# Attention, online memory and a routed FFN on one core: the merge's end reordered, the experts' slot rows transposed by DMA

## Chip, cores, metric

The kernel runs on one core of a Trainium2 chip. The metric is the device time of one execution in microseconds (us); three runs were taken.

## What is computed

```python
def attn(x, mem, ...):                    # x: 8 x 1024 x 256, already layer-normed; mem: 64 x 256
    x_in = concatenate([mem, x], axis=1)
    out_swa = sliding_window_attention(x_in)                # 4 heads, window 128
    grads = grad(0.5 * sum((mlp(x_in) - out_swa) ** 2))     # silu MLP, 256 -> 1024 -> 256
    out_mem = mlp(updated params, x_in)
    g1, g2 = sigmoid(out_swa @ lin1.T), sigmoid(out_mem @ lin2.T)
    return (g1 * out_swa + g2 * out_mem)[:, 64:]

def ffn(h, ...):                          # 8192 tokens, 8 experts, top 2, capacity 640 per expert
    probs = softmax(h @ gate_w.T + gate_b);  top_p, top_i = top_k(probs, 2)
    for c in range(2):                    # dispatch to slots, expert MLP, gather back
        pos = cumsum(one_hot(top_i[:, c])) - 1 at the chosen expert;  keep = pos < CAP
        xbuf[top_i[:, c] * CAP + pos] = h
        yb = relu(xb @ W1[e] + b1) @ W2[e] + b2
        y += yb[slot] * top_p[:, c] * keep

x = x + attn(layernorm(x));  x = x + ffn(layernorm(x))
```

The routed part cuts its tokens off at CAP = 640 slots per expert and choice, as the kernel's constants have it (ROUTED = 2048 tokens give the capacity).

## The kernel before, in words

Four phases follow each other: attention, gradient, merge, experts. Each is a block with its own instruction stream per engine, and a block ends when every engine has drained. All matmuls in f32 are done as three fp32r products of high and low halves (`matmul_split`, line 105): a high half is a rounded copy, a low half is the rest. Whoever wants to multiply needs both halves; ACT usually makes the high one and DVE or POOL the low one. The order of work on each engine is written out by hand; semaphores (`wait_ge`, `then_inc`) join them.

**Merge** (`merge_phase`) goes over 16 chunks C of 512 tokens. Per chunk: eight hidden tiles (`hidden`, products in three PSUM banks `ps_z`), gate1 from `oT`, the memory output `om` (two halves of 128 rows), gate2 of the chunk before. The tail of chunk C-1 runs inside chunk C: second term, merge, `residual` (transposes back to rows, x1), layer norm (x2), `transpose_x2`, `router` (matmuls to 8 logits), and inside chunk C+1 `choose`, `choose_experts`, `dispatch`: softmax, top 8 of the probabilities, counting matmuls, slot numbers. POOL then scatters each row with `routed.scatter` (line 840, indirect DMA) to `xbuf_d`, a row of 256 values and a tail of 4 (token number, two probabilities). x2 is kept in three rotating buffers `routed.rows` of 260 f32, which the scatters read. The last chunk's tail has nothing to hide in. There ACT (from line 2060) and DVE (from line 2281) do the steps in turn, and then make the halves of the first expert's W1 and W2. The last four scatters of merge (`scatter(NCH - 1, 0)`) follow `dispatch(NCH - 1)` on POOL. The eight scatters of the second choice of the last two chunks are the first work of POOL in the expert phase.

**Experts** (`expert_phase`) has 16 rounds i: choice i // 8, expert i % 8, 640 slots in SB = 5 blocks of 128. Per round TensorE does eight `up` tiles (12 products of 320 columns each, L105 into `e_ps_z`) and `down` for five blocks (24 products of 256 columns each, into `e_ps_y`, two banks). In between it transposes the next round's slot rows (`transpose_slots`, line 2496, into `e_ps_x`): blocks 0 to 3 after the first 24 downs, block 4 before the last 24. ACT takes them out of PSUM as the high half (`round_slots`, line 2558), DVE makes the low one (`rest_slots`, line 2609). SP loads W1, the slots (`load_slots`, line 2696, one DMA of 650 KB per round into one of two `slots` buffers) and W2. POOL gathers the output rows of the slots' tokens, DVE adds the weighed result (`weigh`, line 2631), POOL scatters them back. The first round loads its slots in five DMAs (line 2699) and transposes them in three groups before its first up.

In the gradient phase the hidden rows are transposed by DMA: ACT splits f32 words into planes of 16-bit words (line 1213), SP issues a DMA transpose (line 1631), ACT joins them again (line 1219).

## Time and profile before

| | us |
|---|---|
| three runs | 2437.65, 2439.75, 2441.54 (median 2439.75) |
| profiled execution, its time | 2437.23 |
| its span | 2435.4 |
| mean granted TensorE clock | 0.984 |
| busy: TensorE, DVE, ACT, POOL | 2356.8, 1692.9, 1529.5, 1407.8 |
| expert phase, first slot load to the end of the span | 1955.6 to 2435.4 |

The busy time of TensorE is that of the union of its matmuls, which overlap; the rate at which they follow each other is read from starts, or from the pieces of the chain. The granted clock is 1.00 at 2.4 GHz and 0.50 at 1.2 GHz. A name such as PEq or POOLq is an engine's sequencer: waits, branches, issues, drains.

### The profile page before, as it was taken

The page shows a single profiled execution, that of the slowest core. Times are in us where ns is not written, and L with a number is a line of the kernel's source. Part 1 is how long each engine was busy: PE and PEld are TensorE (multiplying, and loading weights), DVE is VectorE, ACT ScalarE, POOL GpSimd, SP SyncE. Part 2 cuts the span into 40 slices and gives each one's busy share as a digit, 9 for nine tenths or more (in the row PEclk, how much of TensorE's full clock was granted, in tenths as well). Part 3 has the DMA queues.
Part 4 walks back from the last instruction along what each step waited for, and adds up shares of the span by engine and source line. Part 5 has one row for each costly group of instructions (what it writes and reads, how often), then busy time and mean ns, then how long its engine had stood idle before and what let it go on. Part 6 is the DMA issues. An engine that isn't in the chain of part 4 may idle for free. (4 is left out here: it accounts for less than half of the span.)

```text
span 2435.4 us, 40493 instructions
## 1 busy us (share of the span) xinstructions
PE 2356.8 (97%) x15170; PEld 2104.4 (86%) x15170; DVE 1692.9 (70%) x3640; ACT 1529.5 (63%) x2390; POOL 1407.8 (58%) x1000
## 2 busy tenths in 40 slices
PE   7999999799999999999999989999999789999998
PEld 6888888688888888888888878888888679999998
DVE  6787776466666666666666766777777657776776
ACT  4787878657777767777776556666656434333333
POOL 2666566556676666667666634666666553333333
PEclk8999999899999999999999999999999889999999
DMA  3222221533333232233222232333222044444441
GB/s 127 81 88 70 92 74 53 222 103 63 69 77 62 61 66 61 64 68 78 61 61 61 72 106 80 102 99 100 91 86 69 22 154 136 139 148 142 136 137 59
DMA packets 260083, 221.76 MB, mean 91 GB/s; under 512 B 138226, under 2 KB 228759, under 8 KB 259760
## 3 DMA queue, kind: packets, MB, share of 16 engines
q1 hardware_dynamic: 246064, 188.73, 27.2%
q0 software_dynamic: 13824, 30.44, 3.7%
q8 instruction: 120, 1.97, 0.3%
q14 instruction: 75, 0.61, 0.1%
HBM read 123.13 MB, written 72.12 MB: 80 GB/s over the span
## 5 line engine op out<-in xcount | busy, mean ns | idle before, releaser
L2314 POOL TENSOR_TENSOR m_hl<-m_hf,m_hh 128x512 fp32r<-128x512 f32 x112 | 158.5, 1421 | 111.6 <-ACT m_hh L1963 110.1
L2675 POOL DMA_INDIRECT out<-e_ys,slot_token x80 | 83.1, 1039 | 223.6 <-DVE e_ys L2631 214.6
L2564 ACT ACTIVATE e_hf<-e_ps_z,e_b 128x640 f32<-128x640 f32 x128 | 101.9, 796 | 145.8 <-PE e_ps_z L105 145.3
L105 PE MATMUL e_ps_y<-r_w_h,e_hl 128*128 128x256 f32 x640 | 180.3, 282 | 0.0
L840 POOL DMA_INDIRECT xbuf_d<-xn,scatter_rows x128 | 153.0, 1195 | 46.4 <-issue 38.1
L105 PE MATMUL e_ps_y<-r_w_h,e_hh 128*128 128x256 f32 x640 | 178.1, 278 | 0.0
L105 PE MATMUL e_ps_y<-r_w_l,e_hh 128*128 128x256 f32 x640 | 177.9, 278 | 0.0
L1565 POOL TENSOR_TENSOR halves_l<-hT_full,halves_h 128x512 fp32r<-128x512 f32 x120 | 153.6, 1302 | 38.3 <-ACT halves_h L1225 38.3
L701 POOL TENSOR_TENSOR prob<-prob,softmax_small 128x1024 f32<-128x1024 f32 x65 | 123.2, 1896 | 72.1 <-DVE softmax_small L634 72.1
L105 PE MATMUL e_ps_z<-slotsT_h,w_l 128*128 128x320 f32 x512 | 159.2, 311 | 1.3 <-DVE slotsT_l L2609 1.3
L105 PE MATMUL e_ps_z<-slotsT_l,w_h 128*128 128x320 f32 x512 | 159.0, 311 | 0.0
L105 PE MATMUL e_ps_z<-slotsT_h,w_h 128*128 128x320 f32 x512 | 158.9, 310 | 0.0
L1423 DVE TENSOR_TENSOR new_w2T<-g_bank,new_w2T 128x512 f32<-128x512 f32 x128 | 88.6, 692 | 93.8 <-PE g_bank L105 93.8
L1219 ACT ACTIVATE hT_full<-h_wordsT 128x2048 uint16<-128x2048 uint16 x60 | 153.1, 2552 | 0.0
L105 PE MATMUL g_bank<-dpred_h,h_l 128*128 128x256 f32 x520 | 148.0, 285 | 2.9 <-DVE shared_x L1416 2.8
L105 PE MATMUL g_bank<-halves_l,keys_h 128*128 128x256 f32 (+1 forms) x528 | 147.8, 280 | 0.0
L105 PE MATMUL g_bank<-dpred_l,h_h 128*128 128x256 f32 x520 | 147.7, 284 | 0.0
L105 PE MATMUL g_bank<-dpred_h,h_h 128*128 128x256 f32 x520 | 147.7, 284 | 0.0
L105 PE MATMUL g_bank<-halves_h,keys_l 128*128 128x256 f32 (+1 forms) x528 | 147.5, 279 | 0.0
L105 PE MATMUL g_bank<-halves_h,keys_h 128*128 128x256 f32 (+1 forms) x528 | 147.3, 279 | 0.0
L1430 DVE TENSOR_TENSOR new_w1T<-g_bank,new_w1T 128x512 f32<-128x512 f32 x128 | 88.5, 692 | 83.6 <-PE g_bank L105 83.6
L1239 ACT ACTIVATE dpredT_h<-dpredT 128x512 fp32r<-128x512 f32 (+1 forms) x33 | 20.7, 627 | 182.6 <-DVE dpredT L1384 178.5
(318 smaller groups left out, 9024.9 us busy)
## 6 DMA issues: line engine op xcount, KB each, us to landing
shared_x<-in_x SPq DMA_DIRECT2D x32, 512.0 KB, 4.9
shared_xT<-xT_d SPq DMA_DIRECT2D x64, 256.0 KB, 4.6
new_w1T<-in_W SPq DMA_DIRECT2D x16, 1024.0 KB, 5.1
new_w2T<-in_W SPq DMA_DIRECT2D x16, 1024.0 KB, 5.7
xbuf_d<-new_w1T SPq DMA_DIRECT2D x16, 650.0 KB, 8.0
slots<-xbuf_d SPq DMA_DIRECT2D x15, 650.0 KB, 6.8
xn_d<-xn SPq DMA_DIRECT2D x32, 256.0 KB, 2.4
xT_d<-shared_xT SPq DMA_DIRECT2D x32, 256.0 KB, 2.6
```

The lines of the kernel that those rows point to most:

```text
L105: i = e.matmul(out, a, b, start=first and not onto and n == 0, stop=last and n == len(terms) - 1, skip_group_check=onto)
L701: e.tensor_tensor(p[:], p[:], sm[:, 3].unsqueeze(2).broadcast_to([P, HEADS, 2 * P]), ALU.mult).then_inc(*prob_made(g))
L840: e.indirect_dma_start(io["xbuf_d"][k], bass.IndirectOffsetOnAxis(ap=self.slot[C % 2][:, k, j:j + 1], axis=0), self.rows[C % 3][:, j], Non ...
L1219: e.activation(hT_f[b][:].bitcast(U16).rearrange("p (n s) -> p s n", s=2), wordsT[b][:].rearrange("p (s k) t -> p s (k t)", s=2), ACTF.Cop ...
L1239: e.activation(dTh[:, :, 0:N], dpf[:, :, 0:N], ACTF.Copy).then_inc(*dT_high(p))
L1423: e.tensor_tensor(dst, bank("g2", p, t)[:], dst, ALU.add).then_inc(*g2_added(p, t))
L1430: e.tensor_tensor(dst, bank("g1", p, t)[:], dst, ALU.add).then_inc(*g1_added(p, t))
L1565: e.tensor_tensor(hTl[:, ks, block[b]], hT_f[b][:, hc].rearrange("p (k t) -> p k t", k=4), hTh[:, ks, block[b]], ALU.subtract).then_inc(*m ...
L2314: e.tensor_tensor(hl[:, t, 0:N], hf[(HC * C + t) % NZ][:, 0:N], hh[:, t, 0:N], ALU.subtract).then_inc(*h_low(C, t))
L2564: e.activation(hf[(HC * i + t) % NHF][:].rearrange("p (s n) -> p s n", s=2), ps_z[t % 2][:, :, 0:HALF], ACTF.Relu, bias=b1[:, i % E, t:t + ...
L2675: e.indirect_dma_start(io["out"], bass.IndirectOffsetOnAxis(ap=token[i % 2][:, b:b + 1], axis=0), ys[:, b], None, bounds_check=NT - 1, oob ...
```

## The change

Merge. A row in `routed.rows` and in `xbuf_d` becomes 520 words of 16 bits: 256 low words, 256 high words, and the tail of 4 f32 as before; the number of bytes is the same. DVE writes x2 to one f32 buffer, and ACT splits it into the planes (`split_x2`), before the second om in a steady chunk. The router takes the top 8 from the logits, so that the expert search no longer waits for the softmax; `shift` makes the differences for all and for the top two, and `weigh` (sum, reciprocal, product of the top two) takes the place of `choose`. The first term moves from the head of the next chunk to the end of its own. In the last chunk om isn't copied as f32 (DVE reads it from PSUM), gate2 goes to banks of its own, W1's halves for the experts are made earlier, W2's high half earlier on ACT, W2's low half in the expert phase, the dispatch of chunk 14 goes ahead of the second term, the sigmoid's table is loaded in advance, and TensorE gets 52 filling matmuls (`keep_busy`) and 8 more at the start of the experts.

Experts. From round 1 on the slot rows are loaded by five DMA transposes and one DMA for the tails, ACT joins the words and rounds them, DVE makes the low half; TensorE transposes nothing. Round 0 loads plain rows, ACT and DVE join the words, and TensorE transposes as before; the first up's first half waits for two groups only. `weigh(i, 1)` goes ahead of the first `rest_slots`.

```diff
         x1 = [sb("x1_0", [P, GRP, D]), shared.oT[:].rearrange("p (j d) -> p j d", j=GRP)]
-        x2 = routed.rows
+        rows = routed.rows
+        x2 = sb("xn2_full", [P, GRP, D])
...
     def gate2_part(C, n):
...
-        acc = bank("gate2", C, n)[:].rearrange("p (m t) -> p m t", m=KC)
+        acc = part_bank(n)[:].rearrange("p (m t) -> p m t", m=KC)
         pe.wait_ge(*om_low.at(C, 1))
-        pe.wait_ge(*freed("gate2", C, n))
+        pe.wait_ge(*h_made.at(C, HC - 1))
...
-    for n in range(2):
-        gate2_part(NCH - 1, n)
-    for n in range(2):
-        residual(NCH - 1, n)
+    def keep_busy(n):
+        for _ in range(n):
+            e.matmul(ps_z[2][:], shared.keys[0][:, 0:P], shared.keys[0][:, 0:512], start=True, stop=True)
+    gate2_part(NCH - 1, 0)
     dispatch(NCH - 2)
+    gate2_part(NCH - 1, 1)
+    keep_busy(2)
+    residual(NCH - 1, 0)
+    keep_busy(2)
+    residual(NCH - 1, 1)
+    keep_busy(12)
     for n in range(2):
         transpose_x2(NCH - 1, n)
     for n in range(2):
         router(NCH - 1, n)
+    keep_busy(4)
     dispatch(NCH - 1)
+    keep_busy(32)
...
+    def split_x2(C, n):
+        blocks = parts_of(C)[n]
+        act.wait_ge(*x2_made.at(C, n))
+        for k in range(TOPK):
+            act.wait_ge(*routed.landed(k, C - 3))
+        e.activation(rows[C % 3][:, blocks, 0:2 * D].rearrange("p j (s n) -> p j s n", s=2),
+                     x2[:, blocks].bitcast(U16).rearrange("p j (n s) -> p j s n", s=2), ACTF.Copy).then_inc(*x2_split(C, n))
...
+        if C == NCH - 1:
+            for k in range(KC):
+                act.wait_ge(*first_w1.at(0))
+                act.wait_ge(*z_done.at(NCH - 1, HC - 1))
+                e.activation(w1h[:, k], g1[:, k], ACTF.Copy).then_inc(*e_w1_high(k))
...
             copy_x2T(C - 1, 0)
+            split_x2(C - 1, 0)
         memory_out(C, 1)
         if tail:
             exponent(C - 1)
+    act.wait_ge(*const_set.at(1))
+    e.activation(spare[:], neg_half[:, 0:1], ACTF.Sigmoid)
     for n in range(2):
         gate2_part(NCH - 1, n)
-    for k in range(KC):
-        act.wait_ge(*first_w1.at(0))
-        act.wait_ge(*z_done.at(NCH - 1, HC - 1))
-        e.activation(w1h[:, k], g1[:, k], ACTF.Copy).then_inc(*e_w1_high(k))
-    for n in range(2):
-        copy_x2T(NCH - 1, n)
-    exponent(NCH - 1)
     for k in range(2):
         r = slice(4 * k, 4 * k + 4)
         act.wait_ge(*first_w2.at(0))
         act.wait_ge(*om_done.at(NCH - 1, 1))
-        e.activation(w2h[:, r], g2[:, r], ACTF.Copy).then_inc(*e_w2_high(k))
+        e.activation(w2h[:, r], g2[:, r], ACTF.Copy)
+    for n in range(2):
+        copy_x2T(NCH - 1, n)
+    for n in range(2):
+        split_x2(NCH - 1, n)
+    exponent(NCH - 1)
...
     def second_term(C, n):
         cols = columns(parts_of(C)[n])
-        dve.wait_ge(*gate2_made.at(C, n if C == NCH - 1 else 1))
-        e.tensor_tensor(gb[:, :, cols], gb[:, :, cols], om[:, :, cols], ALU.mult).then_inc(*term2(C, n))
+        if C < NCH - 1:
+            dve.wait_ge(*gate2_made.at(C, 1))
+            e.tensor_tensor(gb[:, :, cols], gb[:, :, cols], om[:, :, cols], ALU.mult).then_inc(*term2(C, n))
+            return
+        dve.wait_ge(*gate2_made.at(C, n))
+        for m in range(KC):
+            i = e.scalar_tensor_tensor(gb[:, m, cols], bank("om", C, m)[:, cols], b2n[:, m:m + 1], gb[:, m, cols], ALU.add, ALU.mult)
+        i.then_inc(*term2(C, n))
...
     def norm_apply(C, n):
-        y, z, blocks = x1[C % 2], x2[C % 3], parts_of(C)[n]
+        y, blocks = x1[C % 2], parts_of(C)[n]
         dve.wait_ge(*rstd_made.at(C, n))
+        dve.wait_ge(*x2T_done.at(*final_part(C - 1)))
...
+        for j in range(blocks.start, blocks.stop):
+            i = e.tensor_scalar(x2[:, j], y[:, j], mv[:, j, 0:1], rstd[:, 1, j:j + 1], ALU.subtract, ALU.mult)
+        i.then_inc(*x2_made(C, n))
...
-        for j in range(blocks.start, blocks.stop):
-            i = e.tensor_scalar(z[:, j, 0:D], y[:, j], mv[:, j, 0:1], rstd[:, 1, j:j + 1], ALU.subtract, ALU.mult)
-        i.then_inc(*x2_made(C, n))
...
+        for j in range(n):
+            i = e.max(top[:, j], lg[:, j])
+        i.then_inc(*lg_top(C))
+    def shift(C):
+        n, best = SIZES[C], top[:, 0:SIZES[C], 0:1]
+        dve.wait_ge(*lg_top.at(C))
         dve.wait_ge(*exp_made.at(C - 1))
-        e.tensor_tensor(lg[:, 0:n], lg[:, 0:n], mx[:, 0:n].unsqueeze(2).broadcast_to(wide), ALU.subtract).then_inc(*lg_shifted(C))
-    def choose(C):
-        n, wide = SIZES[C], [P, SIZES[C], E]
+        e.tensor_tensor(below[:, 0:n, 0:E], lg[:, 0:n], best.broadcast_to([P, n, E]), ALU.subtract).then_inc(*shifted(C, 0))
+        e.tensor_tensor(below[:, 0:n, E:], top[:, 0:n, 0:TOPK], best.broadcast_to([P, n, TOPK]), ALU.subtract).then_inc(*shifted(C, 1))
...
+    def weigh(C):
+        n = SIZES[C]
         dve.wait_ge(*exp_made.at(C))
...
+        e.tensor_reduce(sm[:, 0, 0:n], pr[:, 0:n, 0:E], AX.X, ALU.add).then_inc(*weighed(C, 0))
+        dve.wait_ge(*weighed.at(C, 0))
+        e.reciprocal(sm[:, 1, 0:n], sm[:, 0, 0:n]).then_inc(*weighed(C, 1))
+        dve.wait_ge(*weighed.at(C, 1))
         dve.wait_ge(*placed.at(C - 1, 7))
...
+        e.tensor_tensor(top_p[:, 0:n], pr[:, 0:n, E:], sm[:, 1, 0:n].unsqueeze(2).broadcast_to([P, n, TOPK]),
+                        ALU.mult).then_inc(*weighed(C, 2))
...
-                choose(C - 2)
+                weigh(C - 2)
...
+        first_term(C)
+        if C == NCH - 1:
+            for k in range(KC):
+                dve.wait_ge(*e_w1_high.at(k))
+                e.tensor_tensor(w1l[:, k], g1[:, k], w1h[:, k], ALU.subtract)
         rest_om(C, 1)
         if tail:
             router(C - 1)
-    choose(NCH - 2)
+            shift(C - 1)
     choose_experts(NCH - 2)
-    first_term(NCH - 1)
+    weigh(NCH - 2)
+    dispatch(NCH - 2)
     for n in range(2):
         second_term(NCH - 1, n)
         merge(NCH - 1, n)
...
         norm_stats(NCH - 1, n)
     for n in range(2):
         norm_apply(NCH - 1, n)
-    dispatch(NCH - 2)
     router(NCH - 1)
-    choose(NCH - 1)
     choose_experts(NCH - 1)
+    shift(NCH - 1)
+    weigh(NCH - 1)
     dispatch(NCH - 1)
...
     def scatter(C, k):
         pool.wait_ge(*placed.at(C, 7))
         pool.wait_ge(*numbered.at(*final_part(C)))
+        pool.wait_ge(*x2_split.at(*final_part(C)))
         routed.scatter(e, io, k, C)
...
-        xs = [sb(f"slots{i}", [P, SB, ROW]) for i in range(2)]
+        tail = [sb(f"slot_tail{i}", [P, SB, ROW - D]) for i in range(2)]
+        words = [sb(f"slot_words{i}", [P, 2 * KC, CAP], U16) for i in range(2)]
+        xf = sb("slotsT_full", [P, KC, CAP])
+        first_words = words[0][:].rearrange("p a t -> p (a t)").rearrange("p (b n) -> p b n", b=SB)
+        first_rows = xf[:].rearrange("p k t -> p (k t)").rearrange("p (b d) -> p b d", b=SB)
...
+    def transpose_first(n):
+        bs, out = groups[0][n], first_bank(n)
         for a, b in enumerate(bs):
-            if i == 0:
-                pe.wait_ge(*first_in[b].at(0))
+            pe.wait_ge(*(act_joined.at(b) if b in by_act else dve_joined.at(b)))
             for m in range(KC):
-                x = e.transpose(out[:, (a * KC + m) * P:(a * KC + m + 1) * P], xs[i % 2][:, b, m * P:(m + 1) * P], ident[:])
-        x.then_inc(*xT_done(i, n))
+                x = e.transpose(out[:, (a * KC + m) * P:(a * KC + m + 1) * P], first_rows[:, b, m * P:(m + 1) * P], ident[:])
+        x.then_inc(*first_T(n))
...
     def up(i, t):
...
-        pe.wait_ge(*xT_low.at(*final_group(i)))
...
         for s in range(2):
+            pe.wait_ge(*xT_low.at(*((0, 1) if (i, s) == (0, 0) else final_group(i))))
...
+    for _ in range(8):
+        e.matmul(ps_z[0][:, 0], w1h[:, 0, 0:P], w1h[:, 0, 0:512], start=True, stop=True)
     for n in range(len(groups[0])):
-        transpose_slots(0, n)
+        transpose_first(n)
     for i in rounds:
         for t in range(HC):
             up(i, t)
         down(i, 0, 0)
         down(i, 1, 0)
-        if i + 1 < ROUNDS:
-            transpose_slots(i + 1, 0)
         down(i, 0, 1)
         down(i, 1, 1)
         for b in range(2, SB):
-            if i + 1 < ROUNDS and b == SB - 1:
-                transpose_slots(i + 1, 1)
             down(i, b, 0)
...
     def round_slots(i, n):
-        bs, src = group_view(i, n)
-        act.wait_ge(*xT_done.at(i, n))
+        cols = slots_of(i, n)
+        act.wait_ge(*slots_in[i % 2].at(i, SB - 1))
+        act.wait_ge(*xT_low.at(*final_group(i - 1)))
+        if i == 1:
+            act.wait_ge(*first_T.at(len(groups[0]) - 1))
+        e.activation(xf[:].bitcast(U16).rearrange("p k (t s) -> p s k t", s=2)[:, :, :, cols],
+                     words[i % 2][:].rearrange("p (s k) t -> p s k t", s=2)[:, :, :, cols], ACTF.Copy).then_inc(*joined(i, n))
+        act.wait_ge(*joined.at(i, n))
         act.wait_ge(*up_done.at(i - 1, HC - 1))
-        e.activation(xh[:].rearrange("p m (b t) -> p m b t", t=P)[:, :, bs], src, ACTF.Copy).then_inc(*xT_high(i, n))
+        e.activation(xh[:, :, cols], xf[:, :, cols], ACTF.Copy).then_inc(*xT_high(i, n))
...
+    def join_first(b):
+        act.wait_ge(*first_in[b].at(0))
+        e.activation(first_rows[:, b].bitcast(U16).rearrange("p (n s) -> p s n", s=2),
+                     first_words[:, b].rearrange("p (s n) -> p s n", s=2), ACTF.Copy).then_inc(*act_joined(b))
+    def round_first(n):
+        bs, src = first_view(n)
+        act.wait_ge(*first_T.at(n))
+        e.activation(xh[:].rearrange("p m (b t) -> p m b t", t=P)[:, :, bs], src, ACTF.Copy).then_inc(*xT_high(0, n))
...
+    join_first(0)
+    join_first(2)
+    round_first(0)
+    join_first(4)
+    round_first(1)
+    round_first(2)
...
     def rest_w2(i, k):
         r = slice(4 * k, 4 * k + 4)
-        dve.wait_ge(*w2_high.at(i, k))
+        if i:
+            dve.wait_ge(*w2_high.at(i, k))
         e.tensor_tensor(w2l[:, r], s2[:, r], w2h[:, r], ALU.subtract).then_inc(*w2_low(i, k))
...
     def rest_slots(i, n):
-        bs, src = group_view(i, n)
+        cols = slots_of(i, n)
         dve.wait_ge(*xT_high.at(i, n))
+        e.tensor_tensor(xl[:, :, cols], xf[:, :, cols], xh[:, :, cols], ALU.subtract).then_inc(*xT_low(i, n))
...
+    for b in by_dve:
+        join_first(b)
     for n in range(len(groups[0])):
-        rest_slots(0, n)
+        rest_first(n)
     slot_tokens(0)
+    for k in range(2):
+        rest_w2(0, k)
...
+        add_bias(i, 1)
+        weigh(i, 1)
         if i + 1 < ROUNDS:
             rest_slots(i + 1, 0)
-        add_bias(i, 1)
-        weigh(i, 1)
...
+        x = x_v[i // E][i % E]
+        for b in range(SB):
+            if i:
+                e.dma_start(words[i % 2][:, :, b * P:(b + 1) * P], x[:, b, 0:2 * D], transpose=True).then_inc(*slots_in[i % 2](i, b))
+            else:
+                e.dma_start(first_words[:, b], x[:, b, 0:2 * D]).then_inc(*first_in[b](0))
+        e.dma_start(tail[i % 2][:].bitcast(U16), x[:, :, 2 * D:]).then_inc(*tail_in[i % 2](i))
```

## Rows read from the trace of the kernel before

**Rows 1.** Page, part 1: engine, busy us (share of span), instructions.
```profile
PE 2356.8 (97%) x15170; PEld 2104.4 (86%) x15170; DVE 1692.9 (70%) x3640; ACT 1529.5 (63%) x2390; POOL 1407.8 (58%) x1000
```

**Rows 2.** Chain of waits, rounds 14 and 15: start us, us, what.
```profile
2386.02 2.72 PE e_ps_y L105 x24
...
2388.75 0.87 PE e_ps_x L2496 x8
...
2389.62 8.49 PE e_ps_y L105 x72
...
2398.11 0.22 PE e_ps_x L2496 x2
...
2398.32 2.73 PE e_ps_y L105 x24
...
2401.05 14.08 PE e_ps_z L105 x96
...
2415.13 13.61 PE e_ps_y L105 x120
```

**Rows 3.** Stretches: length, busy us by engine, PEclk, DMA share, GB/s.
```profile
1940.00:1950.00 10.00, 1.22 (x18) 1.03 (x17) 7.94 (x35) 2.12 (x3) 5.60 (x5) 0.50 0.03 4
...
2010.00:2040.00 30.00, 30.00 (x236) 30.00 (x235) 22.00 (x37) 11.89 (x15) 11.28 (x10) 1.00 0.42 137
```

**Rows 4.** Timeline, merge chunk: start, us, engine, instruction [idle before <-releaser].
```profile
1877.32 0.48 PE L105 MATMUL m_ps_o<-m_hh,r_w_l 128*128 128x512 f32 x1 [0.32 <-ACT gate L1968]
...
1857.46 0.69 ACT L1987 ACTIVATE memT<-m_ps_o,new_b 128x512 f32<-128x512 f32 x1 [1.76 <-PE m_ps_o L105]
```

**Rows 5.** Tile and line views (ns min/median/max), page part 6 (KB, us).
```profile
L1213 ACT ACTIVATE hT_full<-h_full x60: 1912/1913/1916, 519.9 to 1348.2; 128x2048 uint16<-128x2048 uint16 x60
...
L1631 SPq DMA_TRANSPOSE h_wordsT<-hT_full x60: 1317/1890/3135, 521.8 to 1350.1; - x60
...
L1219 ACT ACTIVATE hT_full<-h_wordsT x60: 2529/2551/2574, 529.3 to 1356.3; 128x2048 uint16<-128x2048 uint16 x60
...
DMA to landing us min/median/max: 4.2/4.3/6.0
...
new_w1T<-in_W SPq DMA_DIRECT2D x16, 1024.0 KB, 5.1
...
new_w2T<-in_W SPq DMA_DIRECT2D x16, 1024.0 KB, 5.7
```

**Rows 6.** Timeline of TensorE and DVE at the merge's end.
```profile
1935.29 2.12 PE L1893 MATMUL m_ps_r<-r_ident,xn 128*128 128x128 f32 x8 [3.43 <-DVE xn L2160]
...
1937.20 3.47 PE L1903 MATMUL m_ps_s<-gate_w,xn2T 128*128 128x8 f32 x16
...
1936.22 0.28 DVE L2216 TENSOR_TENSOR router_pos_e<-m_ps_s,expert_counts 128x32 f32<-128x32 f32 x2
...
1937.63 0.16 DVE L2234 TENSOR_TENSOR xn<-router_top,router_keep 128x8 f32<-128x8 f32 x1
...
1940.71 0.19 DVE L2172 TENSOR_TENSOR logits<-m_ps_s,gate_bias 128x32 f32<-128x32 f32 x1 [2.92 <-PE m_ps_s L1903]
...
1940.94 0.19 DVE L2174 TENSOR_REDUCE router_max<-logits 128x4 f32<-128x32 f32 x1
...
1944.68 0.29 DVE L2216 TENSOR_TENSOR router_pos_e<-m_ps_s,expert_counts 128x32 f32<-128x32 f32 x2 [0.64 <-PE m_ps_s L1915]
```

**Rows 7.** Timeline of POOL, the last scatters of merge.
```profile
1947.04 1.20 POOL L840 DMA_INDIRECT xbuf_d<-xn,scatter_rows  x1 [2.04 <-DVE xn L2234]
...
1952.10 0.98 POOL L840 DMA_INDIRECT xbuf_d<-xn,scatter_rows  x1 [0.30 <-issue]
```

**Rows 8.** Line view of the merge's block end.
```profile
L2390 POOLq DRAIN  x1: 6908/6908/6908, 1948.4 to 1948.4; - x1
```

**Rows 9.** Chain of waits, the experts' start.
```profile
1955.61 0.34 SPq L2699
...
1962.22 16.16 PE e_ps_z L105 x96
```

More of the change, by code:

```diff
@@ L826, in __init__ @@
     def __init__(self, sb, sems):
-        self.rows = [sb(f"xn2_{i}", [P, GRP, ROW]) for i in range(3)]
+        self.rows = [sb(f"xn2_{i}", [P, GRP, 2 * ROW], U16) for i in range(3)]
         self.slot = [sb(f"scatter_rows{i}", [P, TOPK, GRP], I32) for i in range(2)]
@@ L832, in __init__, with tails @@
                      for i in range(3)] for k in range(TOPK)]
+    def tails(self, C):
+        return self.rows[C % 3][:, :, 2 * D:].bitcast(F32)
     def landed(self, k, C):
@@ L2329, in gpsimd @@
             e.memset(counts[:], 0.0).then_inc(*const_set(2))
-            for t in x2:
-                i = e.memset(t[:, :, D:], 0.0)
+            for C in range(3):
+                i = e.memset(routed.tails(C), 0.0)
             i.then_inc(*const_set(3))
@@ L2565, in up @@
                              ACTF.Relu, bias=b1[:, i % E, t:t + 1]).then_inc(*h_full(i, t))
-            for n in range(len(groups[0])):
-                round_slots(0, n)
+            join_first(0)
[4 more added lines that the diff above has]
+            round_first(2)
             for i in rounds:
```

163 lines of the change are left out of this document (82 added, 81 removed).

## Prediction, made before the change was run

> **What bounds the kernel now.** I read the shares of the page first: TensorE is busy for 97% of the span [rows 1], so the question for each edit is which TensorE time it removes, and where TensorE waits. Next the chain of waits. From 1962 us to the end it is TensorE alone, round after round of the expert phase: 96 up matmuls, 24 down matmuls, 8 transposes of the next round's slots, 72 down matmuls, 2 transposes, 24 down matmuls [rows 2]. The steps of one round add up to 2.72 + 0.87 + 8.49 + 0.22 + 2.73 + 14.08 = 29.1 us, with no idle in them. Last the table of stretches: between 1940 and 1950 us TensorE is busy for 1.22 us of 10 at the half clock (1.2 GHz); in a round it is busy throughout and the grant is 1.00 [rows 3]. So there are two places where time lies open: the transposes in fifteen rounds, and the seam between merge and experts. In the sixteen merge chunks TensorE waits for only 0.3 us per chunk [rows 4], which is little to win and, since ACT and DVE get new work there, something to lose.
>
> **The transposes in the rounds.** 15 rounds lose 10 transposes each. Their own pieces of the chain are 0.87 + 0.22 = 1.09 us. The row of the last round, which has no transposes, says more: its 120 down matmuls take 13.61 us (0.1134 each), while in a round with transposes the 24 before the first group run at 2.72/24 = 0.1133, the 72 between the groups at 8.49/72 = 0.1179, and the 24 behind them at 0.1138 [rows 2]. The slow pitch begins and ends with the transposes, at a place where DMA traffic hasn't begun yet, so I count it to them: 2.72 + 0.87 + 8.49 + 0.22 + 2.73 = 15.03 against 13.61, 1.42 us per round. 15 x 1.42 = 21.3 us is the value I take, because the last round is the same work without the removed instructions; the bound from the other side is 15 x 1.09 = 16.4 us, if the slow pitch has another cause, such as the neighbours' work in those microseconds.
>
> **What takes their place.** Per round SP issues five DMA transposes of 128 rows x 512 words and one copy of tails, for one copy of 650 KB. The nearest rows are the 60 DMA transposes of the gradient phase, four times as large each (128 x 2048 words): SP is held 1.9 us (3.1 at most) and the data has landed after 4.3 us (6.0 at most) [rows 5]. Lower bound for a slot block: a quarter, 0.5 us of SP; upper bound: the full 3.1 us and 6.0 us. Five of them hold SP for 2.4 to 15.7 us. Behind them on SP's queue is the load of W2 for the next round, which waits for DVE in the middle of the coming ups in any case, and the new slots aren't touched before those ups are over. So they are covered by a round; if that cover went, each microsecond of transfers beyond a round would cost 15. ACT joins the words: 2048 + 512 elements, by the 2.55 us of the same form [rows 5] about 3.2 us per round; its copies into the high halves stay. ACT is busy for 11.9 of 30 us there [rows 3], so it has room, and behind the last up the joins have the 13.6 us of the downs to finish in. DVE's second piece of low halves stays behind the fourth weighing, as now, and no longer waits for a transpose. Cost 0: TensorE has nothing new to wait for at the round's edge.
>
> By a rule of the Trainium skill (VectorE: DVE Perf Modes, "The three transpose paths") a 128 x 128 block of 2-byte words belongs on TensorE where PSUM will do, since the crossbar path takes 1309 ns against 390 ns. Here the 60 transposes moved 16 such blocks each in 4.3 us, 0.27 us per block, so the trace doesn't agree with 1309 ns per block. An estimate from the page's figure, 20 blocks a round, is 26 us per round; slow transposes of that kind are the second rival below.
>
> **The merge chunks.** ACT gets the splitting of x2 between its copy of x2T and the second om. The same form (2048 words, strided in) took 1.91 us [rows 5]. ACT is idle there for 1.76 us [rows 4], so the second om starts about 0.2 us late; with the router's max8 ahead of the shift DVE makes the exponent and the next sigmoids a little later still. Three hidden products are in flight and gate2 lies between the second and the third, so TensorE isn't behind the first sigmoids, and the delay dies out there. The first term leaves the head of the chunk, and weighing loses its four max8. What TensorE waits for, 0.32 us behind gate1 [rows 4], hangs on DVE's work ahead of the sixth hidden product and isn't clearly touched. I take 0; bounds: the wait goes (15 x 0.3 = -4.5 us) or TensorE waits 0.4 us more in each chunk (+6 us).
>
> **The merge's end.** I followed the last chunk to the barrier.
> (a) The sixteen router matmuls take 3.47 us at the half clock [rows 6]. The change puts 16 filling matmuls ahead of them, 12 of these in TensorE's 3.4 us wait for x2 [rows 6]. If the clock is full they take 1.75 us. But the placing of chunk 14 (DVE, 1936.22 to 1937.79, 1.6 us [rows 6]) now comes ahead of the second term, where it is on the path; the first term leaves that path, and x2 comes about 0.4 us later. Net: 0.4 - 1.75 = -1.4 us.
> (b) From the logits (1940.71) to the placing (1944.68) DVE needs 3.97 us, 0.64 of it idle for TensorE's count [rows 6]. The new order searches in the logits, lets TensorE count while DVE shifts and weighs, drops the maximum (0.2 us, as its neighbour of the same size [rows 6]) and adds one shift (0.2 us): 3.97 - 0.64 - 0.2 + 0.2, about -0.6 us. ACT's table load for the exponent lies beside the search.
> (c) The last four scatters start at 1947.04 and the fourth ends at 1953.08 [rows 7]: 6.0 us, 1.20 us for the first of them, while DVE makes its four low halves of the weights; an undisturbed one is 0.98 with 0.30 ahead of it [rows 7]. With W1's halves made earlier and W2's moved into the experts I take 4 x 1.28 = 5.1 us: -0.9 us. POOL's drain, which ends at 1948.4 + 6.9 = 1955.3 us, 2.2 us behind the last scatter, is what the barrier waits for [rows 7, 8]. So (a) to (c), -2.9 us, all count.
> (d) TensorE's 32 filling matmuls behind the last count have 512 columns; by the ups' 320 columns in 14.08/96 = 0.147 us [rows 2] one is 0.235, together 7.5 us at the full clock and 15 at the half. They start near 1942, so they end near 1949.5 to 1951.5 if the clock rises under way, ahead of POOL's drain at some 1952.4; at the half clock throughout they would end at 1957 and take the place of (a) to (c).
> (e) First round: from SP's first issue to the first up 6.6 us (1955.61 to 1962.22) [rows 9]. The joins (ACT or DVE, a quarter of 2.55 us, 0.65) come in ahead of each transpose, but the first up now waits for two groups and not for three: +0.1 us, between -0.5 and +1.5. W2's low halves, now on DVE behind the slots, must be there for the first down, eight ups later: 0.
> (f) The first 96 ups take 16.16 us against 14.08 in a later round [rows 2, 9]: 2.1 us lost to a clock that rises 4 us after their start. Eight filling matmuls and a shorter wait ahead of them should save part: -0.5, between 0 and -2.1. The Trainium skill (TensorE: Matmul & The Clock Gate, Part 4: PE-mode transpose) says that transposes don't count as activity for the full clock; the trace agrees so far, since the ten transposes ahead of the first up left it at half. By that rule (f) would be 0.
> Sum at the seam: -2.9 + 0.1 - 0.5 = -3.3 us, between -6 and +1.
>
> **Sum.** -21.3 + 0 - 3.3 = -24.6 us. The profiled execution took 2437.23 us with a span of 2435.4; it would be 2412.6. The median of the runs shown is 2439.75, 2.5 above it, so the forecast on that scale is 2415.1.
>
> **The rivals.**
> 1. The slow pitch between the transposes isn't theirs: the rounds give 16.4, time 2415.1 + 4.9 = 2420. For it: in those microseconds ACT and DVE work, and ACT gets more to do there. Against it: pitch changes at the transposes to the instruction.
> 2. The other side: DMA transposes out of HBM become the bound. If each of the five runs by itself and takes as long as the longest of the gradient's, 6.0 us [rows 5], that is 30 us; W1 and W2 (5.1 + 5.7 us [rows 5]) run on the same queue, together 40.8 us against a round of 27.7: +13.1 x 15 = +197 us on 2415.1, 2612. It decides from (27.7 - 10.8)/5 = 3.4 us of transfer per slot block of 128 KB. Against it: the gradient's moved four times that in 4.3 us, part of which is the start of a DMA. For it: their source was SBUF, here it is rows of 1040 bytes in HBM. By the page's 1309 ns per block (the Trainium skill, VectorE: DVE Perf Modes, The three transpose paths) the same mechanism would give 26 + 10.8 us a round, 2552.
> 3. TensorE starts to wait in the merge chunks (ACT's 1.91 us, the later exponent): +0.4 us x 15 = 6, 2421. It would show where hidden(6) waits for the fourth hidden product.
> 4. The clock stays at half across the seam and the 32 filling matmuls hold the barrier until 1957.3 in place of 1955.5: 2.9 + 1.8 us dearer, 2420.
> 5. The 0.3 us waits in the chunks vanish as well: 2411.
>
> **How the numbers follow.** Forecast 0.58, rival 1 0.17, rival 2 0.04, rival 3 0.09, rival 4 0.05, rival 5 0.05, and 0.02 that small costs outside these cases eat most of the gain. The forecast's own bounds are 2411 to 2419 (the seam's -6 to +1, a little of the chunks). The range takes in rivals 1, 3, 4 and 5, with 2 us of scatter between runs: 2409 to 2423. A measurement of this kernel can tell 0.2%, 4.9 us, from no change. Faster than 2434.9: all but rival 2 and half of the last case, 0.94; within: 0.02; slower: 0.04.
>
> **What would show it.** Right: 96 + 120 matmuls per round in the chain with nothing between, 14.1 + 13.6 us; rounds of 27.7 us; router matmuls of chunk 15 in about 1.8 us; first slot load near 1952.3 us; SP's transposes landing within 6 us. Wrong: down matmuls still at 0.118 us (rival 1); TensorE waiting for ACT's join at a round's edge, or SP's queue late with W2 (rival 2); waits ahead of hidden(6) (rival 3); TensorE last at the barrier (rival 4).

## The result

The changed kernel takes 2420.07 us (median of 6 runs, 2417.32 to 2422.08) beside 2440.62 (2437.65 to 2441.74) for the kernel before: a ratio of 0.9915, interval 0.9904 to 0.9925, 20.5 us less. (The kernel before has six runs here, three of them shown ahead of the prediction.) The forecast was 2415.1 with a range of 2409 to 2423. The profiled execution of the changed kernel took 2417.32 us, its span is 2415.5.

The page of the changed kernel, its span, the shares, TensorE and the granted clock in 40 slices (before: [rows 1]):

```profile
span 2415.5 us, 40500 instructions
PE 2356.1 (98%) x15080; PEld 2100.2 (87%) x15080; DVE 1691.2 (70%) x3644; ACT 1608.8 (67%) x2439; POOL 1401.9 (58%) x1000
PE   7999999799999999999999989999999989999998
PEclk9999999999999999999999999999999999999999
```

TensorE's busy time has hardly moved though 150 transposes are gone: the 60 filling matmuls are 18.3 us of it. ACT has 79 us more. The chain of waits of the changed kernel, its last rounds (start, duration, what; before: [rows 2]):

```profile
2338.00 14.26 PE e_ps_y L105 x120
2352.26 14.08 PE e_ps_z L105 x96
2366.34 14.27 PE e_ps_y L105 x120
2380.61 14.09 PE e_ps_z L105 x96
2394.69 14.15 PE e_ps_y L105 x120
```

A round is 14.08 + 14.27 = 28.35 us, with no transposes and nothing between, as forecast. But 120 downs take 14.27 us (14.62 in round 4), not 13.61, and even the last round, whose 120 downs took 13.61 before, takes 14.15. I call the time from the start of one down to the start of the next their pitch: 0.113 us is the short one, 0.118 us the long one; where the text says fast or slow of a pitch, it means these two.

I cut the timelines at the same landmarks of TensorE, by the starts of its matmuls; the table also has later experiments, e7 being the kernel before, run again (us; "router 0" is the first router matmul of chunk 0):

| | before | e7 | after | e6 | e9 | e10 | e12 | e11 |
|---|---|---|---|---|---|---|---|---|
| start to first merge matmul | 1412.14 | 1411.30 | 1407.52 | 1411.38 | 1410.11 | 1407.26 | 1410.20 | 1410.34 |
| to router 0 | 58.73 | 59.49 | 58.69 | 59.49 | 58.74 | 58.67 | 58.73 | 59.46 |
| router 0 to 14 | 450.79 | 450.90 | 446.12 | 446.14 | 446.14 | 446.10 | 446.18 | 445.99 |
| router 14 to 15 | 15.54 | 16.76 | 17.28 | 17.00 | 15.17 | 14.30 | 14.32 | 14.31 |
| router 15 to first up | 25.02 | 25.57 | 22.52 | 23.17 | 22.66 | 23.91 | 24.11 | 23.06 |
| first 96 ups | 16.00 | 15.51 | 16.84 | 15.57 | 16.22 | 16.06 | 15.95 | 14.19 |
| first down to last down's end | 450.51 | 454.01 | 439.86 | 430.42 | 439.70 | 439.83 | 437.49 | 431.42 |

So the 19.9 us between the two recorded spans are: 4.6 ahead of the merge, where nothing was changed; 4.7 in the chunks, where I had 0; nearly nothing at the seam (1.74 - 2.50 + 0.84 = +0.1), where I had 3.3; and 10.65 in the rounds, where I had 21.3. The total was in the range; the rounds were outside their bounds (16.4 to 21.3), the chunks just outside theirs (4.5).

**The start.** The first merge matmul stands at 1407.3 to 1412.1 us in all the executions recorded, of either kernel; e2, a variant of the kernel before, has 1408.95. About half of the 4.6 us arises in the first 60 us. The windows there (stretch, length, busy time and count of PE, PEld, DVE, ACT, POOL, granted clock, DMA share, GB/s), first of before, then of after:

```profile
0.00:60.00 60.00, 43.84 (x244) 37.36 (x245) 40.14 (x121) 25.97 (x61) 16.76 (x18) 0.86 0.40 129
...
0.00:60.00 60.00, 45.55 (x271) 39.33 (x272) 43.48 (x125) 28.50 (x70) 18.73 (x19) 0.97 0.41 129
```

The clock was 0.86 in one and 0.97 in the other (0.94 in e6, e7 and e12) under the same instructions. The engines have the same work there, and the ranges of the two kernels overlap (1409.0 to 1412.1 in three traces of the kernel before, 1407.3 to 1411.4 in eleven of the changed kernel and its variants), so I don't count these 4.6 us to the change. The means, 1410.8 and 1409.0, differ by 1.8; three traces are too few to call that nothing.

### The profile page after: what moved, and what is told of

It reads as the page before. It is cut to its first block and busy times, and to the rows that moved or that the text cites. A ratio compares the mean times of both kernels' runs of the same rounds, so it can differ in the third digit from the quotient of the medians.

```text
span 2415.5 us, 40500 instructions
## 1 busy us (share of the span) xinstructions
PE 2356.1 (98%) x15080; PEld 2100.2 (87%) x15080; DVE 1691.2 (70%) x3644; ACT 1608.8 (67%) x2439; POOL 1401.9 (58%) x1000
## 5 line engine op out<-in xcount | busy, mean ns | idle before, releaser
L844 POOL DMA_INDIRECT xbuf_d<-xn,scatter_rows x128 | 147.6, 1153 | 44.5 <-issue 37.8
L1243 ACT ACTIVATE dpredT_h<-dpredT 128x512 fp32r<-128x512 f32 (+1 forms) x33 | 20.7, 627 | 182.4 <-DVE dpredT L1388 178.4
```

Of the source, the lines that this page charges most:

```text
L844: e.indirect_dma_start(io["xbuf_d"][k], bass.IndirectOffsetOnAxis(ap=self.slot[C % 2][:, k, j:j + 1], axis=0), self.rows[C % 3][:, j], Non ...
L1243: e.activation(dTh[:, :, 0:N], dpf[:, :, 0:N], ACTF.Copy).then_inc(*dT_high(p))
```

## Experiments

Five got several runs, and their times stand with them. The others are single executions: e1 2419.84, e2 2434.30, e3 2417.25, e4 2417.72 us beside 2438.89 for the kernel before; e5 2416.07, e7 2442.00, e8 2423.28 beside 2440.40. They are read by their traces.

**e1: disturbances in the downs.** The question was why the downs stay at 0.1179 us. Added to the changed kernel, `kick(i, place)` with:

```diff
+plan = {(2, 1): ("T", 2), (4, 1): ("T", 8), (6, 1): ("T", 1), (8, 1): ("T", 4), (10, 1): ("M", 2), (11, 0): ("T", 2), (12, 2): ("T", 2), (14, 1): ("T", 3)}
+e.transpose(ps_x[...], ident[:], ident[:])       # "T"
+e.matmul(ps_x[...], w2h[:, 0, 0:P], w2h[:, 0, 0:P], start=True, stop=True)   # "M"
```

> The changed kernel with a few extra TensorE instructions into a free bank, written to nothing: two transposes after the first 24 down matmuls of round 2, eight there in round 4, one in 6, four in 8, two plain 128-column matmuls in 10, three transposes in 14; two transposes ahead of the first down of round 11; two ahead of the last 24 downs of round 12. Theory S (the pitch of the downs is a state of TensorE's stream that stays until something sets it; in the kernel before eight transposes set it slow, two set it fast): after round 2's two transposes the rest of that round, 96 downs, and all 120 of round 3 run at 0.1134 us (round 3: 13.6 us of downs), after round 4's eight they are back at 0.118, and so on from round to round. Theory L (the place of the tiles in SBUF or PSUM makes the downs slow in the changed kernel): 0.118 us everywhere, 14.2 us of downs in every round beside the extra instructions' own time. Theory N (neighbours on ACT, DVE and DMA slow them): the same as L except where a neighbour is idle.

Measured: theory L falls, because round 0 ran its downs at 0.113 us here, in the same layout (13.98 us of downs), until round 1. The rule in theory S falls too: two, eight, one, and three transposes left the downs at 0.118; the four in round 8 were followed by 0.113 (14.15 us with the transposes in it). And both times the pitch went back to 0.118, it did so in the middle of a round (1 and 9) behind the 48th down; the same break in round 0 had left it at 0.113. The changed kernel has a small break there, in the timeline of its TensorE (start, duration, what):

```profile
2116.48 0.28 PE L105 MATMUL e_ps_y<-r_w_l,e_hh 128*128 128x256 f32 x1
2116.60 0.28 PE L105 MATMUL e_ps_y<-r_w_h,e_hh 128*128 128x256 f32 x1
2116.75 0.39 PE L105 MATMUL e_ps_y<-r_w_h,e_hl 128*128 128x256 f32 x1
2116.98 0.28 PE L105 MATMUL e_ps_y<-r_w_l,e_hh 128*128 128x256 f32 x1
```

0.15 and 0.23 in place of twice 0.118: 0.14 us, in fourteen of fifteen rounds (14.27 against 14.13). In round 4 the gap was 0.50 us: DVE stood idle for 0.44 us ahead of the weighing, for which the trace names no releaser. The 49th down writes to the bank of block 0, and waits for its weighing. DVE's timeline shows why that is late:

```profile
2113.37 2.35 DVE L2665 TENSOR_TENSOR w_l<-new_w1T,w_h 128x1024 fp32r<-128x1024 f32 x2
2115.64 0.48 DVE L2712 SCALAR_TENSOR_TENSOR token_rows<-e_b,slot_prob,token_rows 128x256 f32<-128x256 f32 x1
2116.21 0.48 DVE L2719 SCALAR_TENSOR_TENSOR e_ys<-e_ps_y,slot_prob,token_rows 128x256 f32<-128x256 f32 x1
```

The weighing stands behind W1's low halves and ends at 2116.69, just ahead of 2116.75.

**e2: the kernel before with fewer transposes.** In `transpose_slots`, after its waits:

```diff
+if skipped(i, n):
+    return
+left_out = [(i, 1) for i in range(5, 9)] + [(i, 0) for i in range(9, 13)] + [(i, n) for i in range(13, 16) for n in range(2)]
```

> The kernel before, without a part of the slot transposes (the rounds concerned compute with stale slots, all other work is kept): loads for rounds 5 to 8 only the group of eight, for 9 to 12 only the group of two, for 13 to 15 none. Theory S: after a group of eight without the group of two behind it the downs stay at 0.118 us, the first 24 of the next round too (2.83 in place of 2.72 us): rounds 5 to 7 have 120 downs at 14.15; with the group of two alone, and without any after it, 0.1134 throughout: 13.6 us of downs, a period of 27.9 and 27.7 us. My prediction's reading (the transposes slow the 72 between them): with one group alone nothing lies between, so 13.6 in all of these rounds. Theory N (ACT and DVE slow the middle of the downs): 8.49 for the middle 72 in every round.

Where a group is left out, the down ahead of it raises its semaphore.

Measured, downs and transposes of a round: 15.23 or 15.24 with both groups in rounds 1 to 3 (the recorded before: 15.03), 15.01 or 15.02 with the eight alone, 14.39 to 14.49 with the two alone, 14.27 with none, 14.15 in the last. In rounds 1 to 3, with both groups, the first 24, the 72 and the last 24 all ran at 0.118. Rounds 12 to 15 have no transposes, and run at 0.118 all the same, round 12 from the break behind its 48th down on. So the slow pitch doesn't need the transposes, and my reading of [rows 2] falls. The 14.27 is the changed kernel's number: take the transposes away and the break behind the 48th down appears, in the kernel before too. The 0.87 us of eight transposes had covered it. At one pitch, removing ten transposes is worth 15.23 - 14.27 = 0.96 us a round.

**e7: the kernel before again,** unchanged.

> The kernel before once more, unchanged. By theory P the pitch of its downs can be another in another execution: rounds of 15.03 us of downs and transposes in the recorded one, 15.23 in a one with the slow pitch throughout, and a last round of 14.1 in place of 13.6; 3 to 4 us in all. If the pitch belongs to the program (its transposes or its layout), 15.03 and 13.6 again. The way to the first merge matmul took 1412.1 us in the recorded execution and 1407.4 to 1409.2 in all others since; I expect 1409 or less, since nothing differs there.

Its chain of waits, one round and the last (compare [rows 2]):

```profile
2360.78 2.83 PE e_ps_y L105 x24
2363.61 0.87 PE e_ps_x L2496 x8
2364.48 8.48 PE e_ps_y L105 x72
2373.18 2.83 PE e_ps_y L105 x24
2376.01 14.08 PE e_ps_z L105 x96
...
2419.40 14.15 PE e_ps_y L105 x120
```

The same program, with the granted clock at 1.00, took 2.83 where it had taken 2.72, and 14.15 where it had taken 13.61: 454.01 us for the rounds in place of 450.51. So the pitch can differ between two executions of one program. The way to the first merge matmul, for which I had expected 1409 us or less, took 1411.30. The runs of the kernel before lie near 2437.8 (two), 2439.75 and near 2441.6 (three), which fits this, without proving it.

**e5: no break, other disturbances.** DVE's order as in e6, below, and one disturbance a round:

```diff
+plan = {(1, 1): ("T", 4), (2, 1): ("T", 4), (3, 1): (64, 1), (4, 1): (128, 1), (5, 1): (192, 1), (6, 1): (32, 1), (7, 1): (256, 1),
+        (8, 1): ("T", 4), (9, 1): (96, 1), (10, 1): (160, 1), (12, 1): (128, 1), (13, 1): ("T", 4), (14, 1): (64, 1)}
```

> The changed kernel with DVE's order in the rounds altered (W1's second low half behind the first weighing, so that the break of about 0.15 us behind the 48th down should go) and one disturbance of TensorE's stream after the first 24 downs of most rounds, into a free bank: four transposes in rounds 1, 2, 8 and 13; one plain matmul of 64 columns in 3 and 14, 128 in 4 and 12, 192 in 5, 32 in 6, 256 in 7, 96 in 9, 160 in 10; nothing in 0, 11 and 15. Theory P (the pitch is a phase that every break of the stream draws anew and that holds until the next break, through the ups too): each stretch between two disturbances has one pitch, 0.1134 or 0.1179 us, round 11 that of round 10's end and 15 that of 14's; no change inside a round other than at the disturbance. Theory L (layout): 0.1179 everywhere. Theory F (four transposes always set the fast pitch): fast after rounds 1, 2, 8 and 13's.

Measured: the half of theory P that says that a pitch holds until the stream is broken. Round 0 had one pitch (13.61 us); it changed only at disturbances: in round 1 the four transposes made it slow, in 2, 8 and 13 four transposes made it fast, in 3, 9 and 14 a plain matmul made it slow, and it passed through the ups in between (13 ended at 0.113, the first 24 of 14 ran at 0.113). Round 11 kept the pitch of 10, round 15 that of 14. Theory F falls with round 1. The other half, that every disturbance draws the pitch anew, isn't shown for the plain matmuls: all nine were followed by the slow one.

**e6: only DVE's order.** The second `add_bias` comes ahead of the first weighing too.

```diff
 if i + 1 < ROUNDS:
-    rest_w1(i + 1)
+    rest_w1(i + 1, 0)
 add_bias(i, 0)
-weigh(i, 0)
 add_bias(i, 1)
+weigh(i, 0)
+if i + 1 < ROUNDS:
+    rest_w1(i + 1, 1)
 weigh(i, 1)
```

> The changed kernel with DVE's order alone altered: W1's second low half behind the first weighing. The break of some 0.15 us behind the 48th down goes in fifteen rounds: -2.2 us against the changed kernel if the pitch stays slow (downs 14.13 us a round, as in the last round now). By theory P the pitch that round 0 starts with then holds to the end: if it is the fast one, 13.6 us a round and -10 us; which of the two is chance, and the runs may fall into two groups some 8 us apart.

2416.04 us (2411.63, 2416.02, 2416.05, 2417.95) beside 2440.4, ratio 0.9902 (0.9885 to 0.9918). The profiled execution is the one of 2411.63; its chain of waits:

```profile
2318.67 14.08 PE e_ps_z L105 x96
2332.75 13.99 PE e_ps_y L105 x120
2346.74 14.08 PE e_ps_z L105 x96
2360.82 14.13 PE e_ps_y L105 x120
2374.95 14.08 PE e_ps_z L105 x96
2389.03 14.15 PE e_ps_y L105 x120
```

Rounds 0 to 12 had 13.60 us of downs each. In round 13 one down came 0.19 us behind the one before it, in place of 0.113, and from there to the end the pitch is 0.118. So the break can be ordered away, and without it the pitch holds.

**e3: no filling matmuls.** In both places:

```diff
-for _ in range(n):        # 52 in the merge; range(8) in the experts
+for _ in range(0):
```

> The changed kernel without any of the 60 filling matmuls. If the fillers do what I priced, the sixteen router matmuls of chunk 15 take 3.5 us in place of about 1.8 to 2.8, the seam from chunk 14's router to the first up grows by 1 to 2 us, and the first 96 ups take 16.2 us or more. Rival: the fillers win nothing at the barrier and cost at the first ups; then the seam is as long (39.8 us) and the first ups take 16.2 us or less, against 16.8 with them.

The rival is right on the barrier, not on the ups. Router matmuls, the last scatter and the first slot load of the changed kernel, then without the fillers:

```profile
1929.61 1.95 PE L1916 MATMUL m_ps_s<-gate_w,xn2T 128*128 128x8 f32 x16
1933.96 9.15 PE L1956 MATMUL m_ps_z<-keys_h 128*128 128x512 f32 x32
1941.51 0.98 POOL L844 DMA_INDIRECT xbuf_d<-xn,scatter_rows  x1 [0.30 <-issue]
1945.01 3.06 SPq L2797 DMA_DIRECT2D slot_words<-xbuf_d  x5
1952.13 0.64 PE L105 MATMUL e_ps_z<-slotsT_h,w_l 128*128 128x320 f32 x1 [0.69 <-DVE slotsT_l L2697]
```

```profile
1929.53 3.42 PE L1916 MATMUL m_ps_s<-gate_w,xn2T 128*128 128x8 f32 x16
1941.99 0.97 POOL L844 DMA_INDIRECT xbuf_d<-xn,scatter_rows  x1 [0.30 <-issue]
1945.50 2.25 SPq L2797 DMA_DIRECT2D slot_words<-xbuf_d  x5
1952.13 0.63 PE L105 MATMUL e_ps_z<-slotsT_h,w_l 128*128 128x320 f32 x1 [0.47 <-DVE slotsT_l L2697]
```

The fillers do make the router's sixteen matmuls faster (1.95 against 3.42 us), but the last scatter is only 0.5 us earlier, and the first up stands at 1952.13 in both, as the five loads' issue took 3.06 us against 2.25 this time. The first ups took 16.84 us with eight fillers, 16.75 without. The whole took 2417.25 us without them; the six runs with them took 2417.32 to 2422.08. One execution can't show a gain or a loss of 1 us here.

**e4 and e8: the 0.32 us in the chunks.** In the changed kernel's chunks no wait of TensorE is listed at all. e4 puts the first term back to the head of the chunk; e8 gives DVE its four max8 back:

```diff
+if tail:
+    first_term(C - 1)
 hidden(C, 0)
...
-first_term(C)
+if C == NCH - 1:
+    first_term(C)
```

```diff
 def weigh(C):
     dve.wait_ge(*exp_made.at(C))
+    for j in range(n):
+        e.max(unused[:, j], pr[:, j, 0:E])
```

> The changed kernel with one edit of the merge undone: the first term's product (DVE) stands again at the head of the next chunk. Theory T: that is what removed the 0.32 us wait in each chunk, so chunks are 32.20 us again (31.87 now), +4.6 us from the first to the last router. Rival: DVE's shorter weighing (no four max8 ahead of the hidden product) removed it; then chunks stay at 31.87 us.

> The changed kernel with four max8 instructions back on DVE in each chunk's weighing (results unused), where the kernel before had them. Theory M: these 0.37 us ahead of the sixth hidden product made ACT's second gate late, for which TensorE waited 0.32 us; chunks are 32.2 us again (31.87 now), +4.5 us from the first to the last router. Rival: they have room, 31.87 stays.

e4: 446.14 us from router 0 to 14, no change. e8: 449.31, +3.2 us. The waits of TensorE there, first of the kernel before, then of e8 (total, times, longest):

```profile
PE m_ps_o L105 <- ACT gate L1968: 4.5, 14, 0.3
...
PE m_ps_o L105 <- ACT gate L1990: 2.8, 14, 0.4
```

So the four max8, 0.37 us of DVE, are the larger part of it: 3.2 of 4.7 us. Both are single executions. What made the rest wasn't tried.

**e10: the placing of chunk 14 in its old place.**

```diff
 weigh(NCH - 2)
-dispatch(NCH - 2)
 for n in range(2):
     second_term(NCH - 1, n)
...
     norm_apply(NCH - 1, n)
+dispatch(NCH - 2)
 router(NCH - 1)
```

> The changed kernel with one edit of the merge's end undone: DVE places chunk 14 again behind the last chunk's normalising, not ahead of its second term. In the changed kernel's record DVE idles 2.0 us ahead of that placing and works 1.6 us on it, and the second term starts behind it. Expected: x2 and the router of chunk 15 some 2.3 us earlier (router 14 to router 15 in 15.0 us in place of 17.3), the scatters of chunk 14 later but hidden, the first up about 2 us earlier, time 2418. Rival: POOL's scatters of chunk 14, five microseconds that now start later, hold those of chunk 15 back; then the first up gains less than 1 us and the time stays at 2420.

Router 14 to 15 took 14.30 us in place of 17.28. DVE's timeline of the changed kernel, and of e10:

```profile
1918.75 0.29 DVE L2273 TENSOR_TENSOR router_pos_e<-m_ps_s,expert_counts 128x32 f32<-128x32 f32 x2 [2.04 <-remote]
1920.24 0.87 DVE L2140 SCALAR_TENSOR_TENSOR gate<-m_ps_o,new_b,gate 128x256 f32<-128x256 f32 x2
```

```profile
1917.12 0.87 DVE L2140 SCALAR_TENSOR_TENSOR gate<-m_ps_o,new_b,gate 128x256 f32<-128x256 f32 x2 [0.70 <-ACT gate L1996]
```

Behind router 14 (1912.33 and 1912.03) the second term starts after 7.9 and 5.1 us, 2.8 earlier. 1.5 us of it is the placing, the rest an idle of 2.04 us ahead of it (0.70 in e10), for which the trace shows no reason on the core, with the counts done at 1916.77; it was 1.68 to 2.04 us in seven traces with this order and 0.10 in the eighth, e9, whose router 14 to 15 took 15.17. Its cause is open. Half of the gain is lost again up to the first up (38.21 us behind router 14, against 39.80); 0.9 us of that stands in the sixteen router matmuls, which took 2.85 us in e10 and 1.95 in the changed kernel. 2415.61 us, where 2418 was expected, beside 2436.56: 0.9922 (0.9906 to 0.9939), not to be told from the changed kernel.

**e9, e11: the pitch set on purpose.** e6 with this in TensorE's order; e11 with e10's edit besides:

```diff
 down(i, 1, 0)
+if i % 5 == 0:
+    e.matmul(ps_x[:, 0:64], w2h[:, 0, 0:P], w2h[:, 0, 0:64], start=True, stop=True)
 down(i, 0, 1)
+if i % 5 == 0:
+    for m in range(4):
+        e.transpose(ps_x[:, m * P:(m + 1) * P], ident[:], ident[:])
```

> The changed kernel with DVE's order as in the third-last experiment (no break in the downs) and the phase of the pitch set on purpose in rounds 0, 5, 10 and 15: one plain matmul of 64 columns after the first 24 downs (so far always followed by the slow pitch), four transposes 12 downs later (so far from slow always to fast, four times of four). Theory P with that rule: rounds 1 to 4, 6 to 9 and 11 to 14 have 13.6 us of downs, the disturbed rounds some 14.2 to 14.4; all executions near the best one of the kernel without the disturbances (2411.6), without its group near 2416. If the four transposes don't set the fast pitch reliably: rounds of 14.13 in part, times spread from 2411 to 2419.

> Both: DVE's order and the set phase in the rounds, and the placing of chunk 14 in its old place. The gains lie in different stages and should add: 2409 us, 11 below the changed kernel, if each gives what it is expected to.

The rule fell: the profiled execution of e9 has 14.13 in every undisturbed round and stays slow behind each four transposes; that of e11, the same instructions in the experts, has 13.60 in every one, and is fast behind each four. 2415.82 (2411.42 to 2417.65), 0.9912 (0.9896 to 0.9929), and 2414.43 (2407.23 to 2416.93), 0.9915 (0.9899 to 0.9932), beside 2436.56. e11's best run is the profiled one, with the short pitch. Its median is 22.1 us below the kernel before, where the expectation (11 below the changed kernel) comes to 31.5: the gains didn't add, and since the other three runs have no trace, why is open.

**e12: e6 and e10, nothing else.**

> DVE's order in the rounds and the placing of chunk 14 in its old place, with nothing put into TensorE's stream. Theory P after the last runs (the pitch is drawn once where the stream starts, holds while nothing breaks it, and no disturbance tried sets it surely): per execution either 14.13 or 13.60 us of downs a round, so two groups some 8 us apart, near 2415 and 2407 beside 2440 for the kernel before; the median belongs to whichever is the more frequent. Against the changed kernel (20.5 us below the kernel before): the removed break gives 2.2 us and the seam 2, 25 us below the kernel before if most executions are slow in pitch, 33 if most are fast. Rival: the gains in DVE's order are eaten elsewhere, 20 to 21 us below the kernel before as now.

2410.31 us (2404.84, 2407.29, 2413.33, 2415.48) beside 2438.04: ratio 0.9879, 0.986 to 0.9897, below the changed kernel's interval, and 27.7 us below the kernel before, between the 25 and 33 expected for the two pitches. The profiled execution is the slowest of these, and has 14.13 us of downs in every round. The spread of 10.6 us, against 4.8 for the changed kernel, is of the size that the two pitches make (16 x 0.53 = 8.5), but the three faster runs have no trace, so that they had the short pitch is argued, not shown.

## Why the prediction was right and where it wasn't

**Rounds, -21.3 forecast.** The step that failed is "I count it to them", and with it the 13.61 us of the last round as the value for the others. The pitch did change at the transposes. Counted over all traces, a group of eight was followed by the long pitch all 39 times; a group of two by the short one in 15 of 15 rounds of the recorded trace, in none of 15 in e7, and in 2 of 8 in e2. But the long pitch needs no transposes (e2's rounds 12 to 15, the changed kernel), and taking them away doesn't bring the short one. The recorded trace had a piece of its chain that spoke against my reading, in round 0: the 24 downs ahead of the first group of eight already took 2.83 us, at a granted clock of 1.00:

```profile
1978.38 2.83 PE e_ps_y L105 x24
1981.21 0.87 PE e_ps_x L2496 x8
```

At one pitch the transposes cost what rival 1 has for them, 1.09 a round (15.23 - 14.13 = 1.10 in e7 and e12, 16.5 us). 2.1 us of it came back as the break behind the 48th down (15 x 0.14) and 0.35 in round 4, which leaves 14.1; 454.01 and 439.86 differ by 14.15. The recorded execution of before had the short pitch in places, 3.5 us better than e7, which leaves the 10.65 of the two traces. My row of the last round was a true one, of an execution with the other pitch. The profiled executions of e6 and e11 reach the sum that I forecast, at 13.60 + 14.08 = 27.68 a round, in their undisturbed rounds.

**"TensorE has nothing new to wait for".** At the round's edge it hadn't; behind the 48th down it had. I had looked at the edge alone, and hadn't asked what the 0.87 us of transposes hid inside the downs.

**SP and DMA transposes.** Right in the main. The five of a round hold SP for 7.8 us, inside my 2.4 to 15.7:

```profile
2115.75 0.37 SPq L2802 DMA_DIRECT2D new_w1T<-in_W  x1
2116.24 7.77 SPq L2795 DMA_TRANSPOSE slot_words<-xbuf_d  x5
2124.06 0.57 SPq L2798 DMA_DIRECT2D slot_tail<-xbuf_d  x1
2136.17 0.37 SPq L2806 DMA_DIRECT2D new_w2T<-in_W  x1
```

W2's load comes 11.5 us after the tail's issue; rival 2 didn't happen. The trace gives no landing for these transposes, so "within 6 us" stays open; from round 1 on no engine's wait for them is listed. ACT's joins are 2.56 and 0.77 us, 3.3 a round for the 3.2 estimated.

**Chunks, 0 forecast, -4.7 measured.** Rival 5, given 0.05. The step that failed is "isn't clearly touched". The text named DVE's work ahead of the sixth hidden product, and the missing max8, in neighbouring sentences, and didn't join them. e8 shows that the 0.37 us of max8 are 3.2 us of the 4.7; the other 1.5 have no cause shown. ACT's new 1.90 us a chunk cost nothing (rival 3 didn't happen).

**Seam, -3.3 forecast.** (a) The router matmuls took 1.95 us, for 1.75 at the full clock, but x2 and the router came 1.7 us later, not 0.4. By e10 the placing of chunk 14 ahead of the second term costs 3.0 us: 1.5 the placing itself, 1.3 more idle time, which I didn't have in the sum. (b) From the logits (1931.60) to the placing (1935.30) 3.70 against 3.97: 0.3 for 0.6. In e7 and e2 the kernel before took 4.90 and 4.88 there, so that one pair says little. (c) The last four scatters took 1937.67 to 1942.49, 4.8 us for 5.1. (d) The fillers end at 1943.11, ahead of the first load at 1945.01: rival 4 didn't happen. (e) First load to first up 7.12 against 6.61: +0.5 for +0.1; over all traces 7.6 in the mean against 6.5, +1.1. (f) 16.84 us, 0.84 more and not 0.5 less. In the first 4 us of these ups the granted clock was 0.50, with the eight fillers ahead of them; in e11, which took 14.19, it was 1.00. Over all traces the means are 16.1 for either kernel (15.51 to 16.89 and 14.19 to 16.97), so the fillers' gain there isn't shown. From router 14 to the first down the kernel before took 56.6, 57.8 (e7) and 59.7 us (e2, the same up to there), mean 58.0; the changed one and the variants that keep the order of its merge's end (e1, e3, e4, e5, e6, e8, e9) 54.1 to 57.1, mean 56.3: a gain of 1.8, less than the scatter among three traces of one kernel, where the recorded pair shows none. The first slot load, forecast for 1952.3 (the sum above gives 1955.6 - 2.9 = 1952.7), came at 1945.01; 9.3 us of that were gained before router 14, so by the seam alone it was 1.6 to 2.0 late.

**Why the total was right.** Its errors cancelled in part, and that is luck. At one pitch and with the mean of the seams the terms are 4.7 (chunks), 14.2 (rounds) and 1.8 (seam), 20.7 us, beside the 20.5 between the medians; the fit isn't as good as it looks, as the start's 1.8 is left out and the pitches of the other runs aren't known. Against these the forecast of 24.6 had 7.1 too much in the rounds, 1.5 too much at the seam and 4.7 too little in the chunks. The measured 2420.07 is rival 1's 2420, which I gave 0.17, and outside the 2411 to 2419 of the forecast proper; the range held it because it took in the rivals.

## What to carry over

Before a difference in pitch between two stretches of one trace is charged to an edit, look whether every round of the trace shows it, the first one too, and whether a second execution of the same program does. When work is taken off the engine that bounds, list the waits of that engine that this work hid, down to the next use of each bank: here 0.87 us of transposes hid a weighing, and a change of DVE's order took the break away again. Where a wait hangs on another engine's chain and an edit shortens that chain, price it: here 0.37 us less of DVE took 0.23 of the 0.33 us per chunk.

## What the runs showed of the hardware

The same 256-column fp32r matmuls, fed without a break at a granted clock of 1.00, follow each other every 0.1133 or every 0.1178 us (13.60 or 14.13 us for 120). A change came only where the stream was broken: a gap of 0.08 us did it once (e6), and the pitch held through hundreds of matmuls, and through the 320-column ups between, whose own pitch (0.147) doesn't show it. What followed a break, counted over all traces: eight transposes, the long pitch 39 times of 39; one plain matmul of 32 to 256 columns, the long one 17 of 17 (7 of these from the short one); the break behind the 48th down never changed the long one (84 times) and changed the short one five times of six; four transposes, the short one in eight places and the long one in five, all alike within e9 (long) and within e11 (short). So nothing tried gave the short pitch for certain. The difference is 0.53 us a round here, 8.5 us in all. What it is physically, no run here tells.
